# One fp32 low-rank-adapter kernel on one core: weight sums stored whole and split later, the low rank part added to the output in SBUF

## The chip, the cores and the metric

The kernel runs on one core of one Trainium2 chip. The metric is the device time of one execution in microseconds (us); the time before is the median of three runs.

## The reference

Two linear layers with residuals, in float32, on 8 batches of 512 tokens with 2048 features. The first takes one of 8 weight matrices by batch, the second takes one shared matrix W, a bias, and a rank 16 adapter by batch.

```python
x = x + einsum('bsi,boi->bso', x, weight[ids0])
base = einsum('bti,oi->bto', x, W) + b
h = einsum('bti,bir->btr', x, lora_As[ids1])
x = x + base + einsum('btr,bro->bto', h, lora_Bs[ids1]) * 2.0
```

## The kernel before

Everything lies transposed: features on the 128 partitions, tokens along the columns. A float32 operand is split into a high part (a ScalarE copy into the type of the fast matmul) and a low part (VectorE: operand minus high part), and a product is three matmuls: high with high, low with high, high with low.

**Phase one** is the first layer: 8 batches of 16 output tiles, `n = 16 b + t`. A tile is 16 k-steps of three matmuls into one bank (48 matmuls), and two more matmuls (`add_h`) gather the rank 16 product h. `x_raw`, `x_hi` and `x_lo` hold one batch in 8 chunks and exist once. So the next batch enters while the last tile of this one is multiplied: PE frees chunk after chunk (`x_free`), ScalarE and VectorE split seven chunks of the next batch, and only then does VectorE add the residual of tile 15 (`x1_sum`, line 681). GpSimd, which issues most DMAs from one queue, stores that tile and its sums (`x1s`, `xss`) and after them loads the eighth chunk, which is split too before PE can go past k-step 13 of the first tile of the next batch.

**Phase two** is the second layer as a two-level Strassen-like scheme: 2 groups of 4 batches, 7 outer products, 7 inner products, 98 stages `s` of 4 tiles, a tile being 12 matmuls. VectorE adds each finished bank into one or two of the quadrants `c_sum` (lines 719, 721; two in five of the seven outer products), splits the x side of the next stage in two halves at m = 1 and 2 (`xc_lo`, line 660), and after m = 3 forms the inner sum of a later stage (`add_terms`), in four stages of seven. SyncE loads one weight tile, `wl`, into five buffers in turn.

The weight sums of phase two are prepared in phase one: 28 units, one in each four tiles n, n < 112. In `split_q` VectorE sums two quadrants of W, then forms seven inner sums; `q_hi` on ScalarE and `q_lo` on VectorE split each, and GpSimd stores high and low parts together, 512 KB (`w1s`). There is one pair of raw buffers; the next unit is loaded in the fourth step and used in the first step after it.

The low rank product of batch b is multiplied during tiles 4 to 11 of batch b + 1, two tiles in each. GpSimd loads x1 back (`xr`), VectorE adds the product and the bias (line 602), GpSimd stores the sum (`cis`), and phase two loads its quadrants from there. For the last batch this happens in stages 4, 5, 11 and 12 of phase two.

Of the kernel before, what the change touches and what calls it, by code (L numbers as in the profile page):

```python
# [5 lines left out]
P = 128  # L6
# [46 lines left out]
INNER = 7  # L53
# [11 lines left out]
SPLIT = [0, 6, 5, 1, 4, 2, 3]  # L65
SPLIT_AT = [(0, 1), (2, 3), (4,), (5, 6)]


def build(nc, xT, ids0, ids1, w0T, w1T, bias, lora_a, lora_b, yT):
# [14 lines left out]
    XR = 4  # L84
    SPLITS = 2

# [5 lines left out]
    cis = scratch("cis", (NB, NT, P, TOK))  # L92
    w1s = scratch("w1s", (PER_GROUP, Q, P, 2, Q, P))
# [9 lines left out]
    def xc_sums(until):  # L103
        return sum(HAS_SUM[s % INNER] for s in range(until))

    with ExitStack() as ctx:
# [8 lines left out]
        with ExitStack() as first:  # L115
# [3 lines left out]
            q_raw = [sb1(f"q_raw{i}", [P, 2, HALF, P]) for i in range(2)]  # L119
            q_out = [sb1(f"q_out{i}", [P, 2, Q, P], F32R) for i in range(2)]  # L120
            sb1("q_rest", [P, 1024])
# [16 lines left out]
            xr = [sb1(f"xr{i}", [P, TOK]) for i in range(XR)]  # L138
# [4 lines left out]
        with ExitStack() as second:  # L143
# [4 lines left out]
            xq = [sb2("xq0", [P, Q, TOK])]  # L148
            xc = [sb2(f"xc{i}", [P, 2, Q, TOK], F32R) for i in range(2)]
# [37 lines left out]
        xr_loaded = [sem(f"xr_loaded{i}") for i in range(XR)]  # L187
        lora_done = sem("lora_done")
        ci_done = sem("ci_done")
        ci_stored = [sem(f"ci_stored{i}") for i in range(XR)]  # L190
        q_loaded = [sem(f"q_loaded{i}") for i in range(2)]
        q_added = sem("q_added")
        q_hi_done = sem("q_hi_done")
        q_ready = sem("q_ready")
        q_stored = [sem(f"q_stored{i}") for i in range(2)]

        xq_loaded = [sem(f"xq_loaded{i}") for i in range(4)]
        wl_loaded = [sem(f"wl_loaded{i}") for i in range(WL)]
        c_loaded = [[sem(f"c_loaded{q}_{i}") for i in range(4)] for q in range(4)]
# [12 lines left out]
        def q_sum_count(u):  # L212

            return sum(len(unit_quads(i)) - 1 + 4 for i in range(u))

        def q_load_count(u, i):
            return sum(len(unit_quads(v)) > i for v in range(u + 1))

        def piece(which):
            return q_raw[0][:, which // 2, which % 2 * Q:(which % 2 + 1) * Q]  # L220


        q_of = [0, 3, 0, 1, 2, 3, 1]

        LORA_FROM, LORA_UNTIL = 4, 4 + NT // 2

        def lora_tiles(b, t):
            if b == 0 or not LORA_FROM <= t < LORA_UNTIL:  # L230
                return []
            return [(t - LORA_FROM) * 2 + i for i in range(2)]

        def late_lora(s):

            return s // INNER < 2 and s % INNER in (4, 5), s // INNER * HALF + (s % INNER - 4) * Q
# [4 lines left out]
        def _(sp):  # L241
# [18 lines left out]
            for i in range(2):  # L260
                sp.wait_ge(q_stored[i], UNITS * INNER // 2 * 16)
            for s in range(SEQ):
                for m in range(Q):
                    n = s * Q + m
                    if n >= WL:
                        sp.wait_ge(acc_done, n - WL + 1)
                    sp.dma_start(wl[n % WL][:].bitcast(F32), w1s[s % PER_GROUP, m]).then_inc(wl_loaded[n % WL], 16)

        @block.gpsimd
        def _(pool):  # L270
# [16 lines left out]

            def load_q(u):
                for i, quad in enumerate(unit_quads(u)):
                    for row in range(2):  # L290
                        tile = quad // 2 * HALF + row * Q + u % Q
                        ks = slice(quad % 2 * HALF, quad % 2 * HALF + HALF)
                        pool.dma_start(q_raw[i][:, row], w1T[tile, :, ks]).then_inc(q_loaded[i], 16)

            def store_q(c):
                u, i = divmod(c, INNER)
                pool.wait_ge(q_ready, c + 1)
                pool.dma_start(w1s[u // Q * INNER + SPLIT[i], u % Q], q_out[c % 2][:].bitcast(F32)  # L298
                               ).then_inc(q_stored[c % 2], 16)

            def load_xr(b, o):
                i = b * NT + o
                if i >= XR:
                    pool.wait_ge(ci_stored[i % XR], i // XR * 16)
                pool.dma_start(xr[i % XR][:], x1s[b, o]).then_inc(xr_loaded[i % XR], 16)

            def store_ci(b, o):
                i = b * NT + o
                pool.wait_ge(ci_done, i + 1)
                pool.dma_start(cis[b, o], xr[i % XR][:]).then_inc(ci_stored[i % XR], 16)  # L310
# [15 lines left out]
            def load_c(group, quad, i):  # L326
                b, t = place_of(group, quad, i)
                pool.dma_start(c_sum[quad][:, i], cis[b, t:t + Q].rearrange("t p n -> p t n")
                               ).then_inc(c_loaded[quad][i], 16)

# [6 lines left out]
            for b in range(NB):  # L337
                for t in range(NT):
# [17 lines left out]
                    if b > 0 and t in (0, 4):  # L356
                        load_b(b - 1, t // 4)
# [3 lines left out]
                    if b > 0 and t == LORA_FROM - 1:  # L361
                        for o in range(2):
                            load_xr(b - 1, o)
                    for o in lora_tiles(b, t):
                        if o + 2 < NT:
                            load_xr(b - 1, o + 2)
                    for o in lora_tiles(b, t):
                        store_ci(b - 1, o)
# [477 lines left out]
```

## Time and profile before

| | us |
|---|---|
| median of 3 runs (2790.5 to 2798.08) | 2792.2 |
| the profiled execution | 2796.53 |
| its span | 2794.9 |
| PE (matmul) busy | 2606.3 |
| VectorE busy | 1681.6 |
| ScalarE busy | 757.8 |
| GpSimd busy | 807.2 |

The span runs from the first to the last instruction. Matmuls overlap, so the busy time of PE says only where it was not idle; how many matmuls start in a stretch says how fast it went. The mean granted clock of TensorE was 0.966 of full speed.

### The profile page before, as it was taken

How to read it: one execution, taken by the hardware profiler on the slowest of the kernel's cores; microseconds unless marked ns; L12 is line 12 of the kernel's file. 1: busy time of each engine (PE TensorE's matmuls, PEld its weight loads, DVE VectorE, ACT ScalarE, POOL GpSimd, SP SyncE). 2: the span in 40 equal slices, each digit the busy share in tenths (PEclk: the TensorE clock that was granted, in tenths of full speed). 3: DMA queues.
4: the chain of work that ended last, by engine and by line, in shares of the span. 5: the costliest groups of instructions: out<-in, count | busy, mean ns of one | idle time of the engine just before them, and what ended most of it. 6: DMA issues, size and time to landing. Idle time of an engine off the chain costs nothing.

```text
span 2794.9 us, 30000 instructions
## 1 busy us (share of the span) xinstructions
PE 2606.3 (93%) x11232; PEld 2140.6 (77%) x11232; DVE 1681.6 (60%) x2020; ACT 757.8 (27%) x961; POOL 807.2 (29%) x1366
## 2 busy tenths in 40 slices
PE   7998998988987999998998998889999999999998
PEld 6887777766866887877876876778888887888887
DVE  5455655545555555555554434568777765677876
ACT  4343333333233343233332221111121121112111
POOL 2324424433442534433532441120010110000112
PEclk9999999998998999999999998999999999999999
DMA  8988988997998998997996998788789996777886
GB/s 310 325 289 310 364 300 296 349 322 244 367 315 269 368 338 289 371 331 252 360 304 183 274 259 305 248 330 311 252 302 354 352 420 233 254 254 252 314 316 256
DMA packets 249316, 848.25 MB, mean 304 GB/s; under 512 B 32340, under 2 KB 32340, under 8 KB 249172
## 3 DMA queue, kind: packets, MB, share of 16 engines
q0 software_dynamic: 155424, 505.50, 53.2%
q1 hardware_dynamic: 93748, 340.84, 33.8%
q8 instruction: 90, 1.47, 0.2%
q14 instruction: 54, 0.44, 0.0%
HBM read 558.90 MB, written 287.31 MB: 303 GB/s over the span
## 4 chain that ended last, share of the span: by engine, by line
PE 58%; DMA 25%; DVE 7%; POOL 4%; issue 2%; ACT 2%; SPq 0%; POOLq 0%; ACTq 0%; DVEq 0%
PE bank L798 12%; PE bank L800 12%; PE bank L802 12%; DMA q_raw<-w1T 9%; DMA w1s<-q_out 8%; PE bank L764 7%; PE bank L765 7%; PE bank L766 7%; DMA x_raw<-xT 2%; DVE x_lo L575 2%; DMA cis<-xr 2%; DVE q_out L608 1%; DMA b_raw<-lora_b 1%; DMA xr<-x1s 1%; ACT q_out L503 1%
## 5 line engine op out<-in xcount | busy, mean ns | idle before, releaser
L764 PE MATMUL bank<-x_hi,w_hi 128*128 128x512 f32 x2048 | 813.0, 397 | 105.4 <-DVE x_lo L575 105.4
L765 PE MATMUL bank<-x_lo,w_hi 128*128 128x512 f32 x2048 | 809.7, 395 | 0.0
L766 PE MATMUL bank<-x_hi,w_lo 128*128 128x512 f32 x2048 | 808.4, 395 | 0.0
L798 PE MATMUL bank<-xc,wl 128*128 128x512 f32 x1568 | 615.5, 393 | 41.6 <-DVE xc L660 31.0
L800 PE MATMUL bank<-xc,wl 128*128 128x512 f32 x1568 | 614.3, 392 | 0.0
L802 PE MATMUL bank<-xc,wl 128*128 128x512 f32 x1568 | 613.7, 391 | 0.0
L764 PEld LDWEIGHTS bank<-x_hi,w_hi 128*128 128x128 f32 x2048 | 392.8, 192 | 192.9 <-DVE x_lo L575 73.1
L765 PEld LDWEIGHTS bank<-x_lo,w_hi 128*128 128x128 f32 x2048 | 393.1, 192 | 82.5
L766 PEld LDWEIGHTS bank<-x_hi,w_lo 128*128 128x128 f32 x2048 | 392.3, 192 | 83.4
L514 ACT ACTIVATE xc<-xq 128x1024 fp32r<-128x1024 f32 x196 | 196.7, 1051 | 885.0 <-DVE xq L650 303.0
L719 DVE TENSOR_TENSOR c<-bank,c 128x512 f32<-128x512 f32 x448 | 298.1, 687 | 216.5 <-PE bank L802 204.8
L798 PEld LDWEIGHTS bank<-xc,wl 128*128 128x128 f32 x1568 | 297.0, 189 | 105.4 <-issue 32.6
L802 PEld LDWEIGHTS bank<-xc,wl 128*128 128x128 f32 x1568 | 297.0, 189 | 62.4
L800 PEld LDWEIGHTS bank<-xc,wl 128*128 128x128 f32 x1568 | 297.2, 190 | 61.7
L453 ACT ACTIVATE w_hi<-w_raw 128x1024 fp32r<-128x1024 f32 x256 | 256.3, 1048 | 268.1 <-PE bank L766 257.3
L569 DVE TENSOR_TENSOR w_lo<-w_raw,w_hi 128x1024 fp32r<-128x1024 f32 x256 | 301.6, 1219 | 37.7 <-ACT w_hi L453 37.7
L503 ACT ACTIVATE q_out<-q_raw 128x512 fp32r<-128x512 f32 x196 | 120.3, 627 | 729.4 <-DMA w1s<-q_out 264.0
L298 POOL DMA_DIRECT2D w1s<-q_out x196 | 109.1, 557 | 577.7 <-DVE q_out L608 575.4
L608 DVE TENSOR_TENSOR q_out<-q_raw,q_out 128x512 fp32r<-128x512 f32 x196 | 132.7, 689 | 227.5 <-ACT q_out L503 227.4
L660 DVE TENSOR_TENSOR xc<-xq,xc 128x1024 fp32r<-128x1024 f32 x196 | 238.3, 1217 | 11.5 <-ACT xc L514 11.5
L681 DVE TENSOR_TENSOR x_raw<-bank,x_raw 128x512 f32<-128x512 f32 x128 | 88.0, 688 | 200.2 <-PE bank L766 199.9
L721 DVE TENSOR_TENSOR c<-c,bank 128x512 f32<-128x512 f32 x224 | 148.3, 683 | 65.0 <-PE bank L802 64.9
(47 smaller groups left out, 1742.4 us busy)
## 6 DMA issues: line engine op xcount, KB each, us to landing
wl<-w1s SPq DMA_DIRECT2D x392, 512.0 KB, 5.8
w_raw<-w0T SPq DMA_DIRECT2D x256, 512.0 KB, 8.4
w1s<-q_out POOLq DMA_DIRECT2D x196, 512.0 KB, 8.3
xss<-x_raw POOLq DMA_DIRECT2D x256, 256.0 KB, 8.1
q_raw<-w1T POOLq DMA_DIRECT2D x96, 512.0 KB, 12.2
xq<-xss POOLq DMA_DIRECT2D x40, 1024.0 KB, 10.4
x1s<-x_raw POOLq DMA_DIRECT2D x128, 256.0 KB, 5.5
xr<-x1s POOLq DMA_DIRECT2D x128, 256.0 KB, 9.3
```

Of the source, the lines that this page charges most:

```text
L453: act.activation(w_hi[s][:, ks], w_raw[s][:, ks], ACT.Copy).then_inc(w_hi_done, 1)
L514: act.activation(xc[s % 2][:, 0, ks], xq[place][:, ks], ACT.Copy).then_inc(xc_hi_done, 1)
L569: dve.tensor_tensor(w_lo[s][:, ks], w_raw[s][:, ks], w_hi[s][:, ks].bitcast(F32), ALU.subtract).then_inc(w_ready, 1)
L608: dve.tensor_tensor(q_out[c % 2][:, 1], piece(q_of[SPLIT[i]]), q_out[c % 2][:, 0].bitcast(F32), ALU.subtract).then_inc(q_ready, 1)
L660: dve.tensor_tensor(xc[s % 2][:, 1, ks], xq[PLACE[s % INNER]][:, ks], xc[s % 2][:, 0, ks].bitcast(F32), ALU.subtract).then_inc(xc_ready, 1)
L719: op = dve.tensor_tensor(tile, bank[m][:], tile, ALU.add)
L764: pe.matmul(sums[s][:], w_hi[s][:, k, :], x_hi[:, k, :], start=(k == 0), stop=False)
L765: pe.matmul(sums[s][:], w_hi[s][:, k, :], x_lo[:, k, :], start=False, stop=False)
L766: mm = pe.matmul(sums[s][:], w_lo[s][:, k, :], x_hi[:, k, :], start=False, stop=(k == KT - 1))
L798: pe.matmul(bank[m][:], w[:, 0, k, :], x[:, 0, k, :], start=(k == 0 and BEGIN[j]), stop=False, skip_group_check=not BEGIN[j])
L800: pe.matmul(bank[m][:], w[:, 0, k, :], x[:, 1, k, :], start=False, stop=False, skip_group_check=not BEGIN[j])
L802: mm = pe.matmul(bank[m][:], w[:, 1, k, :], x[:, 0, k, :], start=False, stop=(k == Q - 1), skip_group_check=not BEGIN[j])
```

## The change

- Weight sums. Phase one stores each of the seven sums whole (256 KB) as soon as it is formed. ScalarE's and VectorE's splitting there is gone. There are three raw buffers, and the next unit is loaded in the second of the four steps.
- In phase two SyncE loads a whole sum into the low half of `wl`; ScalarE writes the high half (`wl_hi`), and GpSimd replaces the low half by the difference (`wl_lo`, a `tensor_tensor` of 128 x 512), 392 times each. PE waits for GpSimd's.
- Low rank part. Phase one splits and stores the h and B operands of each batch (`hs` 8 times, `bs` 16 times); `xr` and `cis` are gone, and the quadrants are loaded from `x1s`. In 16 stages of each group, PE multiplies one low rank tile after each tile into a bank that is free then, and VectorE adds it with the bias to the quadrant in SBUF (128 in all; 16 before in phase two).
- The inner sums of x1 stay on VectorE, in two halves, each with its own semaphore count.
- At the start of phase two four c loads are issued, then four more at n = 5, n = 9 and n = 13. The stores of y are whole stages, one stage later, except in the last stage.

```diff
-            q_raw = [sb1(f"q_raw{i}", [P, 2, HALF, P]) for i in range(2)]
-            q_out = [sb1(f"q_out{i}", [P, 2, Q, P], F32R) for i in range(2)]
+            q_raw = [sb1(f"q_raw{i}", [P, 2, HALF, P]) for i in range(3)]
...
+            hm = sb2("hm", [P, TOK], F32R)
+            bm = [sb2(f"bm{i}", [P, P], F32R) for i in range(BM)]
...
+            def wl_hi(n):
+                act.wait_ge(wl_loaded[n % WL], (n // WL + 1) * 16)
+                if n >= WL:
+                    act.wait_ge(acc_done, n - WL + 1)
+                act.activation(wl[n % WL][:, 0], wl[n % WL][:, 1].bitcast(F32), ACT.Copy).then_inc(wl_hi_done, 1)
...
+            def wl_lo(n):
+                pool.wait_ge(wl_hi_done, n + 1)
+                w = wl[n % WL]
+                pool.tensor_tensor(w[:, 1], w[:, 1].bitcast(F32), w[:, 0].bitcast(F32), ALU.subtract
+                                   ).then_inc(wl_ready, 1)
...
+                        if step == 1 and u + 1 < UNITS:
+                            pool.wait_ge(q_stored, u * INNER * 16)
+                            load_q(u + 1)
...
+                if n == 5:
+                    for i in (0, 3, 1, 2):
+                        load_c(0, 0, i)
+                if n == 8:
+
+                    store_h(NB - 1)
+                    pool.wait_ge(h_stored, NB * 16)
+                    pool.wait_ge(b_stored, NB * 2 * 16)
...
+            for n in range(3, SEQ * Q):
+                s, m = divmod(n, Q)
+                wl_hi(n)
+                if m >= 2 and s + 1 < SEQ:
+                    xc_hi(s + 1, m - 2)
+                if n == 4:
+                    h_hi(NB - 1)
...
+            def add_low_rank(i, bank):
+
+                b, o, quad, inner, m = low_rank_place(i)
+                dve.wait_ge(low_rank_done, i + 1)
+                dve.wait_ge(c_loaded[quad][inner], (i // LOW + 1) * 16)
+                tile = c_sum[quad][:, inner, m]
+                dve.scalar_tensor_tensor(out=tile, in0=bank[:], scalar=bias_sb[:, o:o + 1], in1=tile, op0=ALU.add,
+                                         op1=ALU.add).then_inc(low_rank_added, 1)
...
-                    pe.wait_ge(wl_loaded[n % WL], (n // WL + 1) * 16)
+                    pe.wait_ge(wl_ready, n + 1)
...
+                        pe.matmul(bank_y[m][:], bm[i % BM][:], hm[:], start=True, stop=True
+                                  ).then_inc(low_rank_done, 1)
```

Where instructions stand. ScalarE, the end of tile 14 and the start of tile 15 of batch 0. Before, with the splitting of the weight sum (`q_out`) between the last part of tile 14 and the chunks of the next batch (`x_hi` of 128 x 1024):

```order
L490 ACTIVATE x_hi<-x_raw 128x512 [waits h_part,x1_sum]
L493 ACTIVATE x_neg<-x_raw 128x512 [waits x1_stored0]
L503 ACTIVATE q_out<-q_raw 128x512 [waits q_stored1,q_added,q_loaded0]
L460 ACTIVATE x_hi<-x_raw 128x1024 [waits x_loaded0,x_free]
L460 ACTIVATE x_hi<-x_raw 128x1024 [waits x_loaded1,x_free]
```

The same place now (lines of the changed kernel):

```order
L523 ACTIVATE x_hi<-x_raw 128x512 [waits h_part,x1_sum]
L526 ACTIVATE x_neg<-x_raw 128x512 [waits x1_stored0]
L493 ACTIVATE x_hi<-x_raw 128x1024 [waits x_loaded0,x_free]
L493 ACTIVATE x_hi<-x_raw 128x1024 [waits x_loaded1,x_free]
```

The wait for a stored weight sum that stood ahead of the chunks is gone. GpSimd at the start of phase two, before:

```order
L328 DMA c<-cis 128x4x512 [waits tile_done]
L328 DMA c<-cis 128x4x512 x7
L282 TENSOR_LOAD ids_sb [waits b_ready]
L282 ISA x2
L284 ISA
L284 DMA b_raw<-lora_b 16x1024 x8
L305 DMA xr<-x1s 128x512 [waits ci_stored0]
```

And now, with the differences of nine weight tiles among the loads:

```order
L360 DMA c<-x1s 128x4x512 [waits tile_done]
L360 DMA c<-x1s 128x4x512 x3
L366 TENSOR_TENSOR wl<-wl 128x512 [waits wl_hi_done] x3
L360 DMA c<-x1s 128x4x512 x4
L366 TENSOR_TENSOR wl<-wl 128x512 [waits wl_hi_done] x3
L327 DMA hs<-h_mix 128x512 [waits h_ready]
L366 TENSOR_TENSOR wl<-wl 128x512 [waits x1_stored1,x1_stored0,wl_hi_done,b_stored,h_stored]
L360 DMA c<-x1s 128x4x512 x4
```

The ninth difference (n = 8) stands ahead of the store of h; the tenth waits until that store has landed. VectorE in a stage of two quadrants with a low rank part, its tiles m = 0 and 1, before:

```order
L719 TENSOR_TENSOR c<-bank,c 128x512 [waits acc_done]
L721 TENSOR_TENSOR c<-c,bank 128x512
L719 TENSOR_TENSOR c<-bank,c 128x512 [waits acc_done]
L721 TENSOR_TENSOR c<-c,bank 128x512
L660 TENSOR_TENSOR xc<-xq,xc 128x1024 [waits xc_hi_done]
```

And now:

```order
L743 TENSOR_TENSOR c<-bank,c 128x512 [waits acc_free,acc_done]
L745 TENSOR_TENSOR c<-c,bank 128x512
L632 SCALAR_TENSOR_TENSOR c<-bank,bias_sb,c 128x512 [waits c_loaded0_0,low_rank_done,acc_free]
L743 TENSOR_TENSOR c<-bank,c 128x512 [waits acc_free,acc_done]
L745 TENSOR_TENSOR c<-c,bank 128x512
L632 SCALAR_TENSOR_TENSOR c<-bank,bias_sb,c 128x512 [waits c_loaded0_0,low_rank_done,acc_free]
L682 TENSOR_TENSOR xc<-xq,xc 128x1024 [waits xc_hi_done]
```

One more instruction of 128 x 512 stands in each tile, ahead of the split that the next stage needs.

## Rows read from the trace of the kernel before

**Rows 1.** Tile view of the banks on PE: instruction, count, ns, first and last start

```profile
L764 PE MATMUL bank<-x_hi,w_hi x2048: 387/389/795, 16.5 to 1659.3; 128*128 128x512 f32 x187
...
L798 PE MATMUL bank<-xc,wl x1568: 387/389/796, 1660.5 to 2784.1; 128*128 128x512 f32 x196
```

**Rows 2.** Timeline of PE, 39.9 to 51.4 us: start, length, engine, line; [idle before]

```profile
40.00 0.39 PE L744 MATMUL bank<-x_hi,a_mix 128*128 128x512 f32 x1
...
51.34 0.39 PE L744 MATMUL bank<-x_hi,a_mix 128*128 128x512 f32 x1
```

**Rows 3.** Waits of PE over the span: us in total, times, longest

```profile
PE bank L764 <- DVE x_lo L575: 105.4, 14, 16.5
PE bank L798 <- DVE xc L660: 31.0, 4, 9.3
PE bank L744 <- DVE x_lo L686: 30.2, 9, 7.0
PE bank L798 <- DVE h_mix L588: 10.5, 1, 10.5
```

**Rows 4.** Window 1900 to 2000 us, all engines: busy (instructions), clock, DMA share, GB/s

```profile
1900.00:2000.00 100.00, 100.00 (x443) 82.79 (x442) 79.25 (x98) 18.08 (x18) 5.22 (x7) 1.00 0.78 272
```

**Rows 5.** Timeline of VectorE at 601 us

```profile
601.95 2.29 DVE L619 TENSOR_TENSOR q_raw<-q_raw 128x2048 f32<-128x2048 f32 x1 [15.42 <-DMA q_raw<-w1T]
```

**Rows 6.** Timelines of ScalarE, VectorE, GpSimd, PE, end of batch 2 (620 to 652 us)

```profile
624.49 0.63 ACT L503 ACTIVATE q_out<-q_raw 128x512 fp32r<-128x512 f32 x1 [9.77 <-DMA w1s<-q_out]
...
632.04 2.35 DVE L575 TENSOR_TENSOR x_lo<-x_raw,x_hi 128x1024 fp32r<-128x1024 f32 x2
634.31 0.68 DVE L681 TENSOR_TENSOR x_raw<-bank,x_raw 128x512 f32<-128x512 f32 x1
...
637.50 1.61 POOL L272 DMA_DIRECT2D x_raw<-xT  x1
...
651.79 0.79 PE L764 MATMUL bank<-x_hi,w_hi 128*128 128x512 f32 x1 [12.77 <-DVE x_lo L575]
```

**Rows 7.** Timelines of VectorE and PE, end of batch 0

```profile
206.26 0.68 DVE L681 TENSOR_TENSOR x_raw<-bank,x_raw 128x512 f32<-128x512 f32 x1
...
219.33 0.79 PE L764 MATMUL bank<-x_hi,w_hi 128*128 128x512 f32 x1 [9.84 <-DVE x_lo L575]
```

**Rows 8.** Window 219 to 221 us, all engines, columns as in rows 4

```profile
219.00:221.00 2.00, 1.67 (x4) 1.39 (x5) 1.48 (x3) 0.44 (x1) 0.54 (x1) 0.50 0.04 8
```

**Rows 9.** Timeline of VectorE, start of phase two

```profile
1679.71 1.29 DVE L719 TENSOR_TENSOR c<-bank,c 128x512 f32<-128x512 f32 x2 [11.61 <-DMA c<-cis]
```

**Rows 10.** Chain that ended last, pieces in phase two: start, us, what

```profile
1672.82 36.16 DMA b_raw<-lora_b
...
2296.17 26.19 DMA xq<-xss
```

**Rows 11.** Page, part 6, a DMA issue: size, median us to landing

```profile
c<-cis POOLq DMA_DIRECT2D x32, 1024.0 KB, 22.3
```

**Rows 12.** Window 1690 to 1695 us, all engines, columns as in rows 4

```profile
1690.00:1695.00 5.00, 5.00 (x24) 4.14 (x23) 3.40 (x4) 0.00 (x0) 0.00 (x0) 1.00 1.02 420
```

**Rows 13.** Groups of instructions by line, shapes apart: busy us, mean ns | idle before

```profile
L719 DVE TENSOR_TENSOR c<-bank,c 128x512 f32<-128x512 f32 x448 | 298.1, 687 | 216.5 <-PE bank L802 204.8 <-DMA c<-cis 11.6
...
L660 DVE TENSOR_TENSOR xc<-xq,xc 128x1024 fp32r<-128x1024 f32 x196 | 238.3, 1217 | 11.5 <-ACT xc L514 11.5
L608 DVE TENSOR_TENSOR q_out<-q_raw,q_out 128x512 fp32r<-128x512 f32 x196 | 132.7, 689 | 227.5 <-ACT q_out L503 227.4
...
L602 DVE SCALAR_TENSOR_TENSOR xr<-bank,bias_sb,xr 128x512 f32<-128x512 f32 x128 | 90.9, 745 | 72.0 <-DMA xr<-x1s 71.8
...
L650 DVE TENSOR_TENSOR xq<-xq 128x2048 f32<-128x2048 f32 x28 | 63.9, 2283 | 0.0
```

**Rows 14.** Timeline of VectorE in a stage of two quadrants

```profile
2523.82 0.69 DVE L719 TENSOR_TENSOR c<-bank,c 128x512 f32<-128x512 f32 x1 [0.30 <-PE bank L802]
```

More of the change, by code:

```diff
@@ L210, in unit_quads, with q_sum_count, q_load_count, piece @@
             return [quad for quad in A_SUM[u // Q][:2] if quad is not None]
[L212 to L236, printed above, removed]
+        def q_sum_count(u, step):
+            return sum(len(unit_quads(i)) - 1 + 4 for i in range(u)) + (step > 0) * (len(unit_quads(u)) - 1) + (
+                0, 0, 2, 3, 4)[step]
+        def q_load_count(u, buf):
+            return sum((v + i) % 3 == buf for v in range(u + 1) for i in range(len(unit_quads(v))))
+        def piece(u, which):
+            return q_raw[u % 3][:, which // 2, which % 2 * Q:(which % 2 + 1) * Q]
+        q_store = [[(0, 0), (6, 1), (5, 3)], [(1, 3), (4, 2)], [(2, 0)], [(3, 1)]]
+        Q_STORES = [3, 5, 6, 7]
         block = ctx.enter_context(nc.Block())
@@ L292, in load_q, with store_q @@
                         ks = slice(quad % 2 * HALF, quad % 2 * HALF + HALF)
[L293 to L310, printed above, removed]
+                        pool.dma_start(q_raw[buf][:, row], w1T[tile, :, ks]).then_inc(q_loaded[buf], 16)
+            def store_q(u, step):
+                if step == 0:
+                    pool.wait_ge(q_loaded[u % 3], q_load_count(u, u % 3) * 2 * 16)
+                pool.wait_ge(q_added, q_sum_count(u, step + 1))
+                for j, which in q_store[step]:
+                    pool.dma_start(w1s[u // Q * INNER + j, u % Q], piece(u, which)).then_inc(q_stored, 16)
             def load_xq(outer, q):
@@ L427, in _ @@
-                if group == 1:
-                    for m in range(Q):
+                if n in (9, 13):
+                    for i in (0, 2, 1, 3):
+                        load_c(0, (1, 2)[n // 13], i)
+                if step == 1 and s >= 1:
+                    for done, load in ((s - 1, False), (s - 3, True)):
+                        if not 0 <= done < SEQ:
+                            continue
+                        done_outer, done_j = divmod(done, INNER)
+                        group, o = divmod(done_outer, OUTER)
+                        i = INNER_INTO[done_j]
@@ L615, in split_q, with sum_q @@
+            def sum_q(u, step):
+                a = [piece(u, which) for which in range(4)]
                 if step == 0:
-                    dve.wait_ge(q_loaded[0], q_load_count(u, 0) * 2 * 16)
+                    dve.wait_ge(q_loaded[u % 3], q_load_count(u, u % 3) * 2 * 16)
                     if len(unit_quads(u)) > 1:
-                        dve.wait_ge(q_loaded[1], q_load_count(u, 1) * 2 * 16)
-                        dve.tensor_tensor(q_raw[0][:], q_raw[0][:], q_raw[1][:], A_SUM[u // Q][2]).then_inc(q_added, 1)
@@ L701, in _ @@
                             xc_lo(0, h)
-            add_terms(1)
+            for h in range(SPLITS):
+                add_terms(1, h)
             for h in range(SPLITS):
@@ L729, in _ @@
                     if m == Q - 1:
-                        add_terms(s + 2)
-                    if m == Q - 1 and s in (1, INNER + 1):
-                        b_lo(NB - 1, s // INNER)
+                        for h in range(SPLITS):
+                            add_terms(s + 2, h)
         @block.tensor
```

311 lines of the change are left out of this document (144 added, 167 removed).

## The prediction

> **What bounds the kernel now.** I first read where PE starts and ends in each phase. Phase one takes matmuls from 16.5 to 1660.5 us, phase two from there to 2784 us [rows 1]. A matmul of full speed is priced from two `add_h` matmuls that stand 50 matmuls apart: 11.34 us, so 0.2268 us each [rows 2]. Phase one has 8 x 16 x 50 + 112 = 6512 matmuls, which is 1476.9 us; it took 1644.0, so 167 us are lost. Phase two has 98 x 4 x 12 + 16 = 4720, or 1070.5 us; it took 1124, so 53.5 us are lost. The window inside phase two confirms this: PE is never idle, at clock 1.00, while VectorE is busy 79 of 100 us and DMA 0.78 [rows 4]. In its steady part phase two can't gain; it can only be disturbed.
>
> The waits of PE say where the 220 us are. All are waits for VectorE, though VectorE is busy 60% of the span, so the next question is what made VectorE late [rows 3]. In phase one there are three kinds.
>
> The first is the wait for x1's low part (L744, nine times, 30.2 us). Ahead of one of them VectorE stood 15.42 us for a weight load that was issued one step before it was needed, with everything for PE queued behind [rows 5].
>
> The second and third are the waits of L764: 105.4 us, of which 16.5 is the start of the kernel, so 88.9 lie at the seven batch changes. At batch 2 to 3 ScalarE waited 9.77 us for the store of a weight sum, with the chunks of the next batch behind it. VectorE's seven chunk splits came late, tile 15's residual add came behind these at 634.31, GpSimd could issue the load of the last chunk at 637.50 only, and PE resumed at 651.79 [rows 6]. From the residual add to PE is 17.5 us here, and 13.1 us at the change after batch 0 [rows 7]. The long form belongs to the batches whose last tiles are stored with two adding stores before the load (2, 3 and 6), the short form to the other four.
>
> After each stop the clock is at half for some microseconds: in the first two after 219 us the clock stands at 0.50 and four matmuls start where full speed gives nearly nine [rows 8]. I charge 2 us a stop.
>
> **The change, phase one.** ScalarE and VectorE lose 196 operations each, and the waits for stores of sums that stood before them. The weight loads are issued three tiles earlier, 3 x 50 x 0.2268 = 34 us, against 15.4 us of late arrival: the L744 waits go, 30.2 us.
>
> A new wait can take their place. VectorE's second step now waits until the three stores of the first have landed, and the stores of x1's tiles share that queue. The first step ends about 6 us into its tile, the second comes about 14.6 us after the same point, and if the stores take longer VectorE stands for a few microseconds. PE is two tiles ahead in weights, and x1's low part is made before that step, so it costs nothing up to about 6 us of wait; beyond that each would cost PE what it exceeds.
>
> At a batch change VectorE has, counted from the end of tile 14: residual add and two weight splits, x1's low part, one sum, in all 5.3 us; seven chunk splits, each 1.15 us apart [rows 6], 8.1 us; so the residual add of tile 15 at 13.4 us. Tile 15 ends at 48 x 0.2268 = 10.9, so the add is 2.5 us behind. PE has 42 matmuls, 9.5 us, before it needs the last chunk. It will stand 2.5 + 17.5 - 9.5 = 10.5 us three times and 2.5 + 13.1 - 9.5 = 6.1 us four times, 55.9 in all, with 14 us of half clock, and 2 at the start: 72 us instead of 167, a gain of 95. The path behind the residual add I leave at its price; if the halved stores shorten it, up to 10 us more come back.
>
> The 112 low rank matmuls leave phase one, -25.4 us, and enter phase two, +25.4. Phase one ends at 1660.5 - 25.4 - 95 = 1540.
>
> **The change, phase two.** It begins with 1070.5 + 25.4 = 1095.9 us of matmuls.
>
> What goes: the wait behind the late load of B, 36.16 us to landing, the waits behind the loads and stores of `xr` and `cis`, and the one at the group change, where an x load took 26.19 us to land [rows 10]. There the queue held y and c transfers while SyncE's 512 KB tiles took their share; a tile of 256 KB each 2.72 us frees 96 GB/s of the 420 that the chip moved when full [rows 12]. These are the 31.0 us of waits on L660, with their slow clock.
>
> What stays: the first quadrant load. VectorE stood 11.61 us for it and PE behind that 10.5 [rows 3, 9]. The load is issued at the same place. With half clock 12 us.
>
> What is new at the start: GpSimd must store h and see it landed (n = 8) before it may split the tenth weight tile. Eight c loads of 1 MB stand ahead of that store; they took 22.3 us at the median and more for the last [rows 11]. Phase two starts at T. PE resumes after h at about T + 21.7 and has five tiles, to T + 35.3. The second four c loads are issued near T + 15 and land near T + 38 at 3 us per MB, the store a microsecond behind, then one difference: T + 40. So a stop of some 5 us, 2 more when four further loads are issued between differences, and the half clock: 9 us, between 0 and 15.
>
> Then 392 differences on GpSimd. The trace has no elementwise work of GpSimd on tiles. The bounds are the same shape on VectorE, 0.689 us, and its longest elementwise row, 2.283 us [rows 13]. Either is under the 2.72 us of a tile, and the five buffers give each tile 10.9 us for load, copy and difference. So by itself it is hidden. If GpSimd were to fill, PE would wait for it directly.
>
> VectorE is the tight one. In a tile with two quadrants and a split, it is idle 0.30 us of 2.72 [rows 14]. A low rank add, 0.745 us, makes such a tile 3.1 to 3.2 us against 2.72 + 0.23 with PE's extra matmul. The second half of `xc_lo` then ends 0.45 us after the next stage begins; PE needs it after six matmuls, 1.36 us, so 0.9 us remain (1.56 us in stages with two quadrants and no low rank part). 24 stages are of the first kind, 46 of the second. In the fourth tile the inner sums make VectorE about 2 us late, which the following stage, without sums, gives back. Two splits per stage can be held up by GpSimd's operation if both want one access to SBUF. Held up in full twice by 0.689 us, a stage of the first kind loses 0.5 us, 12 in all. Held up twice by 2.283 us, the first kind loses 3.7 and the second 3.0: 227 us at worst. Below, nothing. I take 10 us, nearest to the same shape, since a hold-up is on average half an operation.
>
> The loads of `bm` (64 KB, three ahead) have 8 us each and cost nothing unless DMA is full.
>
> Phase two: 1095.9 + 12 + 9 + 10 = 1127, against 1124 now. It pays back nothing: the gain is that of phase one.
>
> By the Trainium skill, SBUF — State Buffer, "Who interferes with whom", a VectorE operation with two SBUF inputs and a GpSimd operation that reads SBUF exclude each other for their whole length, and an operation with one input from PSUM is free of this. No row before can show it. By its GPSIMD Engine Reference, section 3, a GpSimd `tensor_tensor` takes 1.96 times VectorE's; with the row of 0.689 us this is an estimate of 1.35 us. Together, two hold-ups of half that length are 1.35 us against 0.9 of slack, 11 us in the 24 stages, and the sum stays as it is; two of full length would be 43 us in the 24 stages and 52 in the 46, and the sum 2760.
>
> **The sum.** 1540 + 1127 + the 10.4 us between the last matmul and the end = 2677 of span, and 1.6 outside it: 2679 against 2796.5 of the profiled execution. The median of the runs is 4.3 us below that execution, so I forecast 2675.
>
> **The rivals.**
> - *Forecast (0.62):* 2650 to 2700.
> - *VectorE late in phase two (0.18).* The low rank adds and the hold-ups exceed the slack in most of the 70 stages, with a half clock behind the longer stops. At 1 us a stage this is 70 us instead of 10, 2735; it reaches from 2700 to 2785. For it speaks the 0.30 us of idle time; against it, that a late PE gives VectorE its time back.
> - *Turns on SBUF fill phase two: slower (0.06).* The place is `wl_lo` against VectorE's two-input operations. These take 238.3 us (L660) and 56 x 2.283 = 128 for the inner sums, 366 together [rows 13]. If GpSimd takes 2.283 us, 895 + 366 = 1261 us exceed the 1096 of matmuls, phase two takes 1273, and the kernel 2675 + 146 = 2821. It decides against the change from (1244 - 366) / 392 = 2.24 us on, where phase two has eaten the 117 us.
>   By the estimate of 1.35 us from the Trainium skill's GPSIMD Engine Reference, section 3, the two would take 529 + 366 = 895 us, and this doesn't happen.
> - *Phase one gives less (0.06).* The stores of the sums hold VectorE longer than 6 us, or PE stands as long as now because the path behind the residual add grows: half of the 95 us go, 2722.
> - *More (0.08).* No stop for the store of h, none in the stages, and a shorter load at the batch changes: 2675 - 9 - 10 - 10 = 2646, down to 2640.
>
> **Numbers.** The range 2645 to 2735 takes in the forecast, the first half of the second case, and most of the fourth and fifth. A change of 0.3% is about what a measurement of this kernel can tell. Slower holds the third case, 0.06; same 0.02 from the upper end of the second; faster the rest, 0.92.
>
> **What would show it.** L744 without waits; seven stops of PE in phase one, of 6 and 10 us; ScalarE ahead of PE at the batch changes; phase two starting near 1540; one stop at its start for the first c load and one behind the store of h; no stop for B, `xr`, or at the group change; `wl_lo` under 1.5 us and PE's waits on it few. The forecast is wrong if `wl_lo` is above 2 us, if PE waits on L682 in more than a third of the stages, or if VectorE stands long at its second step of a unit.

## The result and the profile after

The changed kernel takes 2670.8 us (median of 4 runs, 2668.8 to 2681.8) against 2793.6 before: a ratio of 0.957 (0.954 to 0.960, the 95% interval, as behind every ratio below). The profiled execution has a span of 2668.5 us at a mean granted clock of 0.988 (0.966 before). The forecast was 2675.

The tile view of the banks on PE says where each phase ends (instruction, count, ns, first and last start):

```profile
L783 PE MATMUL bank<-x_hi,w_hi x2048: 387/389/796, 16.4 to 1525.1; 128*128 128x512 f32 x187
...
L812 PE MATMUL bank<-xc,wl x1568: 387/389/794, 1526.2 to 2656.9; 128*128 128x512 f32 x196
```

Against [rows 1], phase one ends 134.3 us earlier and phase two takes 1130.7 us instead of 1123.6, although it has 25.4 us more matmuls. The waits of PE after the change, to set beside [rows 3]:

```profile
PE bank L783 <- DVE x_lo L604: 60.8, 8, 16.4
...
PE bank L812 <- DVE h_mix L617: 8.4, 1, 8.4
...
PE bank L812 <- POOL wl L366: 7.5, 4, 4.7
...
PE bank L812 <- DVE xc L682: 4.1, 7, 1.4
...
PE bank L830 <- DMA bm<-bs: 2.8, 4, 0.9
```

L783 is the former L764: the 105.4 us are now 60.8, and 16.4 of that is the kernel's start. The waits for x1's low part (30.2 us at L744) are gone. The four long waits on the x side in phase two (31.0 us) are gone too; there are seven short ones. Two kinds are new, for GpSimd's differences (`wl`, L366) and for the B tiles (`bm`). The two long stops of phase two stand at its start: 8.4 us for h and 4.7 us for the tenth weight tile.

The page's lines for the differences, for VectorE's additions to c and for its splits of the x side:

```profile
L366 POOL TENSOR_TENSOR wl<-wl 128x512 fp32r<-128x512 f32 x392 | 587.1, 1518 | 459.0 <-ACT wl L532 444.5
...
L743 DVE TENSOR_TENSOR c<-bank,c 128x512 f32<-128x512 f32 x448 | 296.7, 683 | 126.9 <-PE bank L816 119.1
...
L682 DVE TENSOR_TENSOR xc<-xq,xc 128x1024 fp32r<-128x1024 f32 x196 | 328.0, 1674 | 0.3 <-ACT xc L543 0.2
```

Of the 459.0 us that GpSimd is idle ahead of its differences, it waits 444.5 for ScalarE, so it is no bound. But the split on VectorE, 1217 ns in [rows 13], is 1674 ns now (means). This is an instruction that the change did not touch. The addition to c, with one input from PSUM, is as it was (687 ns before, 683 now).

### The profile page after: what moved, and what is told of

Read it like the earlier page. It is cut to its first block, busy times and chain, and to the rows that moved or that the text cites. A ratio compares the mean times of both kernels' runs of the same rounds, so it can differ in the third digit from the quotient of the medians.

```text
span 2668.5 us, 30970 instructions
## 1 busy us (share of the span) xinstructions
PE 2573.8 (96%) x11232; PEld 2118.8 (79%) x11232; DVE 1664.3 (62%) x1880; ACT 876.2 (33%) x1157; POOL 1247.3 (47%) x1484
## 4 chain that ended last, share of the span: by engine, by line
PE 86%; DMA 6%; DVE 5%; POOL 1%; issue 1%; ACT 1%; SPq 0%; DVEq 0%; ACTq 0%
PE bank L783 16%; PE bank L785 16%; PE bank L784 16%; PE bank L812 12%; PE bank L814 12%; PE bank L816 12%; DMA x_raw<-xT 3%; DVE x_lo L604 2%; DMA bm<-bs 1%; PE bank L768 1%; PE bank L830 1%; PE bank L769 1%; DVE w_lo L598 1%; DMA wl<-w1s 1%; DVE xc L682 1%
## 5 line engine op out<-in xcount | busy, mean ns | idle before, releaser
L783 PE MATMUL bank<-x_hi,w_hi 128*128 128x512 f32 x2048 | 802.4, 392 | 60.8 <-DVE x_lo L604 60.8
L366 POOL TENSOR_TENSOR wl<-wl 128x512 fp32r<-128x512 f32 x392 | 587.1, 1518 | 459.0 <-ACT wl L532 444.5
L784 PE MATMUL bank<-x_lo,w_hi 128*128 128x512 f32 x2048 | 801.0, 391 | 0.0
L783 PEld LDWEIGHTS bank<-x_hi,w_hi 128*128 128x128 f32 x2048 | 387.0, 189 | 144.0 <-DVE x_lo L604 47.3
L784 PEld LDWEIGHTS bank<-x_lo,w_hi 128*128 128x128 f32 x2048 | 387.2, 189 | 80.4
L381 POOL DMA_DIRECT2D x1s<-x_raw x128 | 70.4, 550 | 672.9 <-DVE x_raw L703 672.9
L532 ACT ACTIVATE wl<-wl 128x512 fp32r<-128x512 f32 x392 | 241.2, 625 | 383.4 <-DMA wl<-w1s 374.9
L682 DVE TENSOR_TENSOR xc<-xq,xc 128x1024 fp32r<-128x1024 f32 x196 | 328.0, 1674 | 0.3 <-ACT xc L543 0.2
L543 ACT ACTIVATE xc<-xq 128x1024 fp32r<-128x1024 f32 x196 | 206.4, 1054 | 315.1 <-DVE xq L672 132.7
L342 POOL DMA_DIRECT2D w1s<-q_raw x196 | 109.3, 579 | 223.2 <-DVE q_raw L656 94.3
```

The lines of the kernel that those rows point to most:

```text
L366: pool.tensor_tensor(w[:, 1], w[:, 1].bitcast(F32), w[:, 0].bitcast(F32), ALU.subtract).then_inc(wl_ready, 1)
L532: act.activation(wl[n % WL][:, 0], wl[n % WL][:, 1].bitcast(F32), ACT.Copy).then_inc(wl_hi_done, 1)
L682: dve.tensor_tensor(xc[s % 2][:, 1, ks], xq[PLACE[s % INNER]][:, ks], xc[s % 2][:, 0, ks].bitcast(F32), ALU.subtract).then_inc(xc_ready, 1)
L783: pe.matmul(sums[s][:], w_hi[s][:, k, :], x_hi[:, k, :], start=(k == 0), stop=False)
L784: pe.matmul(sums[s][:], w_hi[s][:, k, :], x_lo[:, k, :], start=False, stop=False)
```

## The experiments

Phase one's end and phase two's length are from the profiled execution of each, worked out from the first phase-two matmul and the last start of the same line. In what follows, "theory" and "rival" are the two cases of the expectation that stands ahead of each result.

| kernel | median us | phase one ends | phase two |
|---|---|---|---|
| before | 2792 to 2796 | 1660.5 | 1123.6 |
| changed | 2670.8 | 1526.2 | 1130.7 |
| e1: weights loaded late | 2674.7 | 1526.5 | 1135.2 |
| e2: sums stored twice | 2679.9 | 1532.3 | 1134.3 |
| e3: differences of 8 columns | 2658.8 | 1526.1 | 1119.5 |
| e4: low rank adds of 8 columns | 2667.9 | 1530.7 | 1124.3 |
| e5: store of h ahead of c loads | 2670.3 | 1527.5 | 1130.3 |
| e6: first c load on SyncE | 2671.3 | 1528.8 | 1126.5 |
| e7: last x chunk ahead of stores | 2615.7 | 1469.7 | 1130.9 |
| e8: e5, e6 and e7 | 2614.8 | 1469.2 | 1128.6 |
| b9: before, three output buffers | 2744.8 | 1612.5 | 1121.0 |
| b10: before, x chunk ahead of stores | 2744.9 | 1607.9 | 1123.1 |
| b11: before, without the xr and cis transfers | 2732.8 | 1603.1 | 1117.2 |
| b12: before, splits of 8 columns | 2778.1 | 1641.2 | 1119.9 |

The changed kernel, e3, e4, e5 and e6 run the same phase one: their ends, 1526.1 to 1530.7, show how much it differs from execution to execution. Phase two does the same work in the changed kernel, e1, e2 and e7, and in e5, e6 and e8 but for the order at its start; it took 1126.5 to 1135.2 us there.

**e1, weights loaded late.** 

```diff
-                        if step == 1 and u + 1 < UNITS:
+                        if step == 3 and u + 1 < UNITS:
```

> The changed kernel, with the next unit of the weight sums loaded in the fourth step again (three raw buffers stay). Theory (the early load took away the waits for x1's low part, 30.2 us in rows 3): VectorE stands some 10 us for the raw weights at the first step of each unit, PE waits on the add_h matmul (L768) again, 20 to 30 us with its half clock, 2690 to 2705. Rival (the queue is so much emptier without the xr, cis and half of the w1s transfers that the load lands in time even when issued late): no waits on L768, 2671 as the changed kernel.

Measured: 2674.7 us, phase one unchanged, no wait for x1's low part. VectorE does stand for the raw weights again, but for 65.7 us in all against 186.7 before, and it costs PE nothing in phase one. The kernel before, then this one:

```profile
DVE q_raw L619 <- DMA q_raw<-w1T: 186.7, 19, 15.9
```

```profile
DVE q_raw L643 <- DMA q_raw<-w1T: 65.7, 19, 6.9
```

The rival held. The 4 us more stand in phase two, which the edit doesn't touch.

**e2, sums stored twice.**

```diff
                     pool.dma_start(w1s[u // Q * INNER + j, u % Q], piece(u, which)).then_inc(q_stored, 16)
+                    pool.dma_start(w1x[u // Q * INNER + j, u % Q], piece(u, which)).then_inc(q_stored, 16)
...
-                            pool.wait_ge(q_stored, u * INNER * 16)
+                            pool.wait_ge(q_stored, u * INNER * 32)
```

> The changed kernel, with each weight sum stored twice (a second scratch tensor that nothing reads), so that phase one writes 512 KB a sum as before, while ScalarE and VectorE split nothing. Theory (phase one gained because ScalarE and VectorE no longer stand for stores ahead of the chunks of the next batch): the batch changes stay at 5 to 9 us, VectorE stands some us at its second step, under 10 us in all, 2671 to 2681. Rival (it gained because half the stores are gone from the queue): stops at the batch changes grow by 3 us or more each and L768 waits, 2700 and more.

Measured: 2679.9 us, 9 more, of which 6 in phase one. There is no wait for x1's low part; the stops at the batch changes differ by about 2 us at most from the changed kernel's. The time lies in the theory's range, but VectorE's waits for these stores at its second step grew from 2.6 to 28.0 us, more than the 10 expected. They were short enough (5.4 us at the most) for PE to feel little of them: the 50 MB of stores cost 6 us of phase one.

**e3, differences of 8 columns.**

```diff
-                pool.tensor_tensor(w[:, 1], w[:, 1].bitcast(F32), w[:, 0].bitcast(F32), ALU.subtract
+                pool.tensor_tensor(w[:, 1, 0, 0:8], w[:, 1, 0, 0:8].bitcast(F32), w[:, 0, 0, 0:8].bitcast(F32), ALU.subtract
```

> The changed kernel, with GpSimd's difference taken over 8 columns instead of 512, so most of the low half of each weight tile stays the whole sum; matmuls, transfers and waits are the same. Theory (GpSimd's 1518 ns operations hold up VectorE's two-input operations, L682 at 1674 ns against 1217 before, and this makes PE's small stops in phase two): L682 falls to about 1217, the x1 sums too, and PE's stops on L682 go; phase two 1131 falls by 5 to 15 us, kernel 2656 to 2666. Rival (VectorE's longer L682 comes from the DMA writes or from ScalarE, or the stops are those of the low rank adds alone): L682 stays at 1674 and the time at 2671.

Measured: 2658.8 us, 12 less, with phase two 11.2 us shorter. The tile view of VectorE's splits (ns: least, median, most), of the changed kernel and then of this one:

```profile
L682 DVE TENSOR_TENSOR xc<-xq,xc x196: 1207/1515/5346, 1496.0 to 2645.4; 128x1024 fp32r<-128x1024 f32 x196
```

```profile
L682 DVE TENSOR_TENSOR xc<-xq,xc x196: 1212/1216/1251, 1495.8 to 2634.1; 128x1024 fp32r<-128x1024 f32 x196
```

Nothing but GpSimd's work was cut, and VectorE's splits are back at one duration, where the changed kernel's reach 5346 ns. No split of this run is longer than 1251 ns, though GpSimd issues the same DMAs, so the stretching comes of the differences. PE's waits on L682 are gone altogether. The theory held, and the price of GpSimd's differences in phase two is measured: 11 us. That is their price in both ways, by holding up VectorE and by coming late themselves (PE's waits on L366 fall too, from 7.5 to 4.8 us); the run doesn't part the two. The tile view of `wl` has GpSimd's own duration in the changed kernel:

```profile
L366 POOL TENSOR_TENSOR wl<-wl x392: 1258/1302/2385, 1520.2 to 2651.1; 128x512 fp32r<-128x512 f32 x196
```

Some of them are stretched as well, to 2385 ns.

**e4, low rank adds of 8 columns.**

```diff
-                dve.scalar_tensor_tensor(out=tile, in0=bank[:], scalar=bias_sb[:, o:o + 1], in1=tile, op0=ALU.add,
+                dve.scalar_tensor_tensor(out=tile[:, 0:8], in0=bank[:, 0:8], scalar=bias_sb[:, o:o + 1], in1=tile[:, 0:8], op0=ALU.add,
```

> The changed kernel, with the low rank add taken over 8 columns instead of 512, so the low rank part and the bias are left out of the other columns; its waits and PE's low rank matmuls stay. Theory (VectorE is only just on time in stages of two quadrants, and the add of 0.745 us uses up the slack): PE's stops on L682 go and VectorE's busy time falls by some 75 us, kernel 3 to 8 us faster, 2663 to 2668. Rival (the stops in phase two are those for GpSimd and for bm alone, which the add doesn't touch): within 2 us of 2671.

Measured: 2667.9 us. Phase two is 6.4 us shorter, and PE's waits on L682 fall from 4.1 to 2.1 us. The medians differ by 3 us, less than executions of one program do, and this phase two is only 2.2 us shorter than the shortest with the whole adds (e6). The stops did not go, as the theory had it; they halved. That the adds take part in them is likely, as the waits on L682 are 3.9 us or more in every run with whole adds and whole differences, but it is not shown beyond that.

**e5, the store of h ahead of four c loads.**

```diff
-                if n == 5:
-                    for i in (0, 3, 1, 2):
-                        load_c(0, 0, i)
...
+                if n == 9:
+                    for i in (0, 3, 1, 2):
+                        load_c(0, 0, i)
+                if n in (13, 17):
...
```

> The changed kernel, with the second four c loads issued behind the store of h (at n = 9; the others at 13 and 17) instead of ahead of it at n = 5. Theory (GpSimd stands 12.5 us for that store because 4 MB of c loads lie ahead of it in its queue, and PE then stops 4.7 us on the tenth weight tile): GpSimd's wait falls under 4 us, the stop goes with its half clock, 2662 to 2666. Rival (the store waits for the writes of x1's last tiles or for h itself): GpSimd's wait stays, 2671.

GpSimd's timeline in the changed kernel (start, length, [idle before]) shows the wait, with four c loads of 1 MB issued ahead of the store:

```profile
1538.41 3.01 POOL L360 DMA_DIRECT2D c<-x1s  x4
...
1552.91 0.58 POOL L327 DMA_DIRECT2D hs<-h_mix  x1
1565.96 1.26 POOL L366 TENSOR_TENSOR wl<-wl 128x512 fp32r<-128x512 f32 x1 [12.48 <-DMA hs<-h_mix]
```

And in this one, the first difference behind the store:

```profile
1555.76 1.54 POOL L366 TENSOR_TENSOR wl<-wl 128x512 fp32r<-128x512 f32 x1 [1.79 <-DMA hs<-h_mix]
```

The wait fell from 12.48 to 1.79 us, and PE's long stop on the tenth tile went: the first low rank matmul starts 56.8 us into phase two instead of 65.3. But the kernel is not faster: at the ninth of those matmuls the lead is 4.5 us (138.8 against 143.3), at the 64th 2.4, and none is left at the 65th. PE's waits on L682 are 8.5 us here against 4.1, and a wait of 2.5 us on L745 is new. That they come of the loads that were put off is not shown. The mechanism held and the forecast of the time did not.

**e6, the first c load on SyncE.** 

```diff
+                    if n == WL:
+                        sp.wait_ge(tile_done, TILES)
+                        sp.wait_ge(x1_sum, TILES)
+                        sp.dma_start(c_sum[3][:, 0], x1s[2, HALF:HALF + Q].rearrange("t p n -> p t n")).then_inc(c_first, 16)
...
-            for i in (0, 3, 1, 2):
+            for i in (3, 1, 2):
                 load_c(0, 3, i)
```

> The changed kernel, with the first c load (1 MB of batch 2) issued by SyncE when the last tile of phase one is done, in place of GpSimd's. Theory (the stop of 8.4 us on h at the start of phase two is the time that the first c load spends behind x and xss transfers in GpSimd's queue, since VectorE adds two tiles to c before it makes h's low part): the c load lands 5 to 8 us earlier, the stop falls under 3 us, kernel 2660 to 2665. Rival (the transfer is slow because the 16 DMA engines are full, on whichever queue): the stop stays over 6 us, 2671.

Measured: 2671.3 us. The wait on h fell from 8.4 to 5.0 us, but a stop of 1.9 us came behind it and the one on a weight tile grew from 4.7 to 6.0. The load still took 13.1 us to land, from the other queue, against 14.0. Most of the 3.4 us come from its issue, which stands 0.5 us behind the first matmul of phase two instead of 3.0. In this stretch the DMA engines were full:

```profile
1529.00:1543.00 14.00, 11.26 (x50) 9.00 (x48) 9.22 (x7) 4.68 (x7) 8.17 (x9) 1.00 1.06 331
```

(The columns are those of rows 4: clock 1.00, DMA share 1.06, 331 GB/s.) So the rival's reason held, the transfer was slow on either queue, and so did its time; the stop itself lies between its 6 us and the theory's 3.

**e7, the last x chunk ahead of the stores of tile 15.**

```diff
                     pool.wait_ge(x1_sum, n + 1)
+                    if b < NB - 1 and t == NT - 1:
+                        load_x(b + 1, t // KX)
                     pool.dma_start(x1s[b, t], x1_raw[s][:]).then_inc(x1_stored[s], 16)
...
-                    if b < NB - 1 and t % KX == KX - 1:
+                    if b < NB - 1 and t % KX == KX - 1 and t < NT - 1:
                         load_x(b + 1, t // KX)
```

> The changed kernel, with the load of the last x chunk of the next batch issued ahead of the stores of tile 15 instead of behind them. Theory (what is left of the stops at the seven batch changes is the path behind the residual add, in which the load stands behind two to four stores, two of them adding): the load is issued 1 to 3 us earlier and lands in 5 to 6 us instead of 8 to 12; the stops fall from 45 us to under 15, all with less half clock, kernel 2630 to 2645. Rival (the load's time is that of full DMA engines, and only the issue moves): stops fall by 1.2 us in four and 3 us in three changes, 14 us in all, 2657.

Measured: 2615.7 us, a ratio of 0.937 (0.935 to 0.940) to before; it beats the changed kernel by 55 us. PE's waits on x are the kernel's start and 0.7 us:

```profile
PE bank L785 <- DVE x_lo L606: 16.9, 2, 16.2
```

Timelines of GpSimd and ScalarE at the change from batch 2 to 3:

```profile
563.96 0.55 POOL L305 DMA_DIRECT2D x_raw<-xT  x1 [7.98 <-DVE x_raw L705]
...
570.02 1.06 ACT L495 ACTIVATE x_hi<-x_raw 128x1024 fp32r<-128x1024 f32 x1 [5.17 <-DMA x_raw<-xT]
```

From the issue to ScalarE's start it is 6.1 us. In the changed kernel the same load is issued 3.2 us behind the start of the residual add instead of 1.0, and ScalarE starts on it 11.1 us after the issue. Over the seven batch changes this load took 8.1 to 11.9 us to land in the changed kernel, behind three or four stores, and 4.4 to 6.0 us here. The theory's mechanism held and its range fell short: all seven stops are gone with their half clock, 56.5 us of phase one. From its first matmul, phase one now takes 1453.5 us, where its 6400 matmuls at 0.2268 us are 1451.5: there is next to nothing left to gain there but by fewer matmuls.

**e8, the edits of e5, e6 and e7 together.**

> The changed kernel with three edits together: the last x chunk loaded ahead of the stores of tile 15, the c loads behind the store of h, the first c load issued by SyncE. The first alone gave 2615.7, the other two nothing that could be told from noise. Theory (PE's stops at the start of phase two, 8.5 and 4.9 us, can be shortened by order, but half of what is won is given back in the stops for full DMA engines and in small stops behind): 2605 to 2613. Rival (all that is won at the start of phase two is given back before its end): 2614 to 2617.

Measured: 2614.8 us (median of 5 runs), 0.936 (0.934 to 0.938), the fastest median. The time lies in the rival's range: the edits at the start of phase two are worth nothing that can be told beside e7.

**b9, the kernel before with three output buffers for the sums.** 

```diff
-            q_out = [sb1(f"q_out{i}", [P, 2, Q, P], F32R) for i in range(2)]
-            sb1("q_rest", [P, 1024])
+            q_out = [sb1(f"q_out{i}", [P, 2, Q, P], F32R) for i in range(3)]
...
-                if c >= 2:
-                    act.wait_ge(q_stored[c % 2], c // 2 * 16)
...
+                if c >= 3:
+                    act.wait_ge(q_stored[c % 3], c // 3 * 16)
```

> The kernel before, with three output buffers for the split weight sums instead of two (the third takes the place of padding). Theory (at the batch changes ScalarE stood for a store of a sum, 9.77 us in rows 6, with the next batch's chunks behind it): with a store more of room ScalarE's waits for w1s, 264 us before, fall under 100, the first stop at a batch change (before the first chunk) goes, and the second grows less than that, 5 to 25 us faster than before. Rival (the chunks were late for VectorE's own work and for the weight load, and the store wait was covered by them): within 3 us of before.

Measured: 2744.8 us, 0.983 (0.981 to 0.986). ScalarE's wait for stores is nearly gone, and with it 48 us of phase one, twice the most that I expected. The kernel before, then this one:

```profile
ACT q_out L503 <- DMA w1s<-q_out: 264.0, 57, 11.4
```

```profile
ACT q_out L502 <- DMA w1s<-q_out: 23.7, 5, 7.1
```

**b10, the kernel before with the order of e7 (the same edit).**

> The kernel before, with the load of the last x chunk ahead of the stores of tile 15. Theory (this path is apart from the splitting of the weight sums, and its order costs 40 us or more with either kernel): 35 to 55 us faster than before, 2740 to 2757. Rival (before, the batch changes are set by ScalarE's wait for the store of a sum, and a load that lands earlier is only waited for less): under 20 us faster.

Measured: 2744.9 us, 0.983 (0.981 to 0.985). The theory held: the order of stores and load costs some 50 us in either kernel.

**b11, the kernel before without the transfers of the low rank part.** 

```diff
-                pool.dma_start(xr[i % XR][:], x1s[b, o]).then_inc(xr_loaded[i % XR], 16)
+                cols = slice(0, TOK if i < XR else 8)
+                pool.dma_start(xr[i % XR][:, cols], x1s[b, o][:, cols]).then_inc(xr_loaded[i % XR], 16)
...
-                pool.dma_start(cis[b, o], xr[i % XR][:]).then_inc(ci_stored[i % XR], 16)
+                pool.dma_start(cis[b, o][:, 0:8], xr[i % XR][:, 0:8]).then_inc(ci_stored[i % XR], 16)
```

> The kernel before, with the loads of x1 for the low rank part (after the first four) and the stores of the sums cut to 8 columns and the quadrants loaded from x1 instead, so the low rank part and the bias are missing from the output; all waits stay. 67 MB of transfers are gone from phase one. Theory (phase one gained through ScalarE's and VectorE's waits, of which emptier queues shorten a part: the stores of the sums land sooner): 10 to 25 us faster than before. Rival (the queue's load is the main cause of the late stores and weight loads): 50 us or more faster. Second rival (no part): within 5 us.

Measured: 2732.8 us, 0.978 (0.975 to 0.980), some 60 us less than before. That is far more than the theory said; the first rival (50 us or more, by the queue's load) held. The waits of VectorE and ScalarE in phase one, and PE's:

```profile
DVE q_raw L620 <- DMA q_raw<-w1T: 139.7, 19, 10.2
ACT q_out L504 <- DMA w1s<-q_out: 110.8, 37, 10.4
PE bank L765 <- DVE x_lo L576: 102.2, 11, 17.0
```

ScalarE's wait for stores is 110.8 instead of 264 us, VectorE's wait for raw weights 139.7 instead of 186.7, and PE has no wait for x1's low part any more. The waits at the batch changes stay, 102.2 us against 105.4 (both with the kernel's start). So 33 us of the 57 that phase one gains are PE's waits, and most of the rest is the slow clock that stood behind them.

**b12, the kernel before with splits of 8 columns.** 

```diff
-                act.activation(q_out[c % 2][:, 0], piece(q_of[SPLIT[i]]), ACT.Copy).then_inc(q_hi_done, 1)
+                k, o = (Q, P) if c < 2 else (1, 8)
+                act.activation(q_out[c % 2][:, 0, 0:k, 0:o], piece(q_of[SPLIT[i]])[:, 0:k, 0:o], ACT.Copy).then_inc(q_hi_done, 1)
...
```

(VectorE's split is cut in the same way.)

> The kernel before, with the splits of the weight sums on ScalarE and VectorE cut to 8 columns after the first two, so phase two multiplies by other values; the sums, the stores of 512 KB and all waits stay. Theory (the waits for stores held ScalarE and VectorE, not their work): 0 to 12 us faster than before. Rival (the work of 120 and 133 us is what made the chunks late): 40 us or more faster.

Measured: 2778.1 us, 0.994 (0.992 to 0.996). It lies between theory and rival, nearer to the theory: the work itself was worth some 18 us. Without it ScalarE stands for the stores even longer, 317.1 us against 264.0.

## Why the prediction was right, step by step

**The bound, and where the loss was.** This was right: a matmul takes 0.2268 us (e7's phase one comes within some 2 us of that rate), and phase two had no room in its steady part. Of the 167 us that phase one lost before, 119 were waits of PE and some 44 the slow clock behind them; in the changed kernel it is 44 and 13.

**Phase one, 1540 against 1526.2.** The mechanism was right for the batch changes. Each of the seven stops is left with one part, the path behind the residual add:

```profile
592.39 0.79 PE L783 MATMUL bank<-x_hi,w_hi 128*128 128x512 f32 x1 [7.99 <-DVE x_lo L604]
```

PE waited 12.77 us there before [rows 6], behind an earlier stop of 3.9 us, and 7.99 now. To set a stop beside the forecast I count the distance of two matmul starts less 0.2268 us, which is 0.16 us more than the idle time in the row. The four short stops are then 4.8 to 5.0 us where I said 6.1, the three long ones 8.2 to 8.9 where I said 10.5, 45.4 in all against 55.9. That is 10.5 of the 14 us, and two terms were off. The residual add starts 1.4 us behind the last matmul of tile 15 where I said 2.5. And PE has 44 matmuls before it needs the last chunk, 10.0 us, where I said 42: I left out the two for h, which stand there too (L768, L769). The path behind the add stayed at its price, 13.4 to 13.6 and 16.7 to 17.5 us against 13.1 and 17.5. The half clock behind the seven stops costs 12.6 us, forecast 14.

**The waits for x1's low part.** They went, 30.2 us. The cause that I read was right: VectorE stands for the raw weights 19 times in the kernel before; behind each of the eight stands of 10.3 to 15.9 us PE waits 1.65 to 7.0 us for x1's low part (29.6 of the 30.2 us), and behind none of the eleven of 10.2 us or less. The remedy that I named, the load issued three tiles earlier, is not needed for it. With the late load put back (e1) the waits don't return; VectorE's longest stand for raw weights is 6.9 us there. In the kernel before they go when only the `xr` and `cis` transfers do (b11), where the longest is 10.2 us. So the loads came late because of what else the queues carried, of which the change takes the same transfers away. The term had the right size for a step that did not decide it, and this was luck. Whether the earlier issue alone would have been enough in the kernel before was not run.

**What the gain is made of.** My working put it to ScalarE's and VectorE's waits ahead of the next batch's chunks and to the weight loads. b9, where ScalarE has one buffer more to store from, gives 48 us of phase one; b11, which thins the queue, gives 57; the work alone gives 19 (b12). The changed kernel gives 134, of which 25 are the low rank matmuls that moved. The three together would be 124 us and the rest is 109, so they overlap; they were not run together, and how the 109 us divide among them is not shown. The thinner queue, with the largest of the three, had no term of its own in my sum. That the path behind the residual add is apart from all this is shown: its order gives 53 us in the kernel before and 56 in the changed one.

**Phase two, 1127 against 1130.7.** The stop for the first c load was forecast at 12 us; it measures 8.5 and 2.8 of half clock behind it. The stop for the store of h was forecast at 9 us; it measures 4.9 and 2.4, with GpSimd's wait as described. The long waits for B, `xr`, `cis` and at the group change are gone, as forecast. For the stops through GpSimd and VectorE I took 10 us; e3 measures 11. The loads of `bm` I had put at nothing; PE waits 2.8 us for them. `wl_lo` takes 1.30 us at the median, between the two bounds of 0.689 and 2.283.

The Trainium skill, SBUF — State Buffer, "Who interferes with whom", says that VectorE operations with two SBUF inputs and GpSimd operations that read SBUF exclude each other. The trace agrees: L682 has two, L682 takes 1515 ns at the median and 1216 in e3, where the differences are cut, while the additions to c with one input from PSUM stay at 683 ns (687 before). By the Trainium skill's GPSIMD Engine Reference, section 3, I had estimated 1.35 us for GpSimd's operation; measured, 1.30.

**The rivals.** VectorE late in phase two by 1 us a stage did not happen: the stops on L682 are seven, of 4.1 us in all. Turns on SBUF that fill phase two would have needed 2.24 us a difference; they take 1.30 at the median. Phase one giving less by VectorE's wait at its second step did not happen either: it stood 2.6 us for stores in all. "More", by a shorter load at the batch changes, was there to be had, but by another order, and it is worth 55 us, not 10. I took the load's time as its own there, and at the change from batch 2 to 3 some 5 of its 11 us were the stores ahead of it.

**What stays open.** Why the gains of e5 and e6 at the start of phase two are given back is not shown, only where e5's are: by the ninth low rank matmul and around the group change. The stretch between the 64th and 65th low rank matmul took 115.6 us in the changed kernel and 114.8 to 120.5 in e1, e2, e5, e6, e7 and e8, all with the same work, so a difference of a few us in phase two can't be told from one profile.

## What to carry to other kernels

When a wait is long, look at what stands ahead of the awaited transfer in its own queue before its own size: one load for each batch, moved ahead of three or four stores, was worth 55 us here, against 123 us for the whole rebuild. Where one engine waits for a store that frees a buffer, everything behind that wait on the engine is late too; a third buffer alone gave 48 us in the kernel before. Work moved to an engine that is idle can still hold up another: compare the duration of untouched instructions before and after.

## What the hardware showed that I had not expected

A VectorE split of 128 x 1024 with two SBUF inputs took up to 5346 ns, four times its 1216, beside GpSimd's differences of 1302 ns at the median. One that started at 1531.86 us lasted 5.08 us, while GpSimd ran two differences:

```profile
1531.86 5.08 DVE L682 TENSOR_TENSOR xc<-xq,xc 128x1024 fp32r<-128x1024 f32 x1 [0.24 <-ACT xc L543]
```

```profile
1532.25 3.60 POOL L366 TENSOR_TENSOR wl<-wl 128x512 fp32r<-128x512 f32 x2
```

It ended about 1.1 us after the second difference, nearly its own length. By these times it was held through both; the two differences were stretched as well, to 3.60 us together. I had priced a hold-up at one operation at the most.

A load of 1 MB took 13.1 us from SyncE's queue at the start of phase two (e6), where 1 MB takes about 2.5 us at the 420 GB/s of [rows 12].
